# Front stage of a mixture-of-experts kernel: routing weights by row transfers instead of a matmul

## The reference, cut to what matters

```python
logits = x @ gate_weight.T                      # 16 experts
scores = sigmoid(logits)
topk_w, topk_idx = top_k(scores, 2)
topk_w = topk_w / (topk_w.sum(-1) + 1e-20)
comb = zeros((T, 16)).at[arange(T), topk_idx].set(topk_w)
g = silu(einsum('th,ehi->eti', x, We_gate))
u = einsum('th,ehi->eti', x, We_up)
ye = einsum('eti,eih->eth', g * u, We_down)
y = einsum('te,eth->th', comb, ye)              # + the shared expert
x = x + 0.5 * (y + shared)
```

## Time and profile before

| | us |
|---|---|
| median of 3 runs | 2211.61 (2210.7 to 2214.48) |
| time of the profiled execution | 2212.05 |
| span of its trace | 2210.3 |
| PE busy | 1984.1 (90%) |
| DVE busy | 1650.0 (75%) |
| ACT busy | 1083.3 (49%) |
| POOL busy | 585.6 (26%) |

### The profile page before, as it was taken

One profiled execution on the slowest core, in us unless ns is written; L12 is line 12 of the kernel. 1 busy time (PEld: TensorE's weight loads), 2 busy tenths in 40 slices (PEclk: granted clock), 3 DMA queues, 4 the chain that ended last, 5 costly groups with the idle time before them and its releaser, 6 DMA issues. The chain is left out here.

```text
span 2210.3 us, 34280 instructions
## 1 busy us (share of the span) xinstructions
PE 1984.1 (90%) x12468; PEld 1352.9 (61%) x12468; DVE 1650.0 (75%) x4096; ACT 1083.3 (49%) x1971; POOL 585.6 (26%) x621
## 2 busy tenths in 40 slices
PE   3998999899989998989899838999999999999997
PEld 3787778777877787778777723344444444444444
DVE  5766776767676767776767518988988888889982
ACT  3333323332333233323332214777777777777775
POOL 3332333233223331333133021222222222222211
PEclk9999999999999999999999956999999999999999
DMA  3000000000000000000000022222222222222220
GB/s 119 6 11 10 1 11 10 11 1 10 11 10 1 10 11 10 1 11 11 10 1 6 5 72 81 73 81 84 78 78 78 78 87 88 78 78 78 73 73 10
DMA packets 49991, 85.81 MB, mean 39 GB/s; under 512 B 6752, under 2 KB 11104, under 8 KB 49760
## 3 DMA queue, kind: packets, MB, share of 16 engines
q1 hardware_dynamic: 47920, 81.85, 11.6%
q10 hardware_dynamic: 1904, 1.78, 0.2%
HBM read 49.26 MB, written 34.87 MB: 38 GB/s over the span
## 5 line engine op out<-in xcount | busy, mean ns | idle before, releaser
L1302 DVE TENSOR_REDUCE b_nm<-b_MX 128x1 f32<-128x512 f32 x1024 | 651.8, 683 | 80.1 <-PE b_MX L1417 71.4
L1184 ACT ACTIVATE b_pr<-b_ST 128x512 f32<-128x512 f32 x1024 | 551.7, 601 | 175.8 <-PE b_ST L1404 173.9
L383 ACT ACTIVATE s<-G 128x512 f32<-128x512 f32 x306 | 182.9, 598 | 432.3 <-PE G L685 423.2
L1417 PE MATMUL b_MX<-b_kt,b_qt 32*128 32x512 f32 x1024 | 357.7, 505 | 20.8 <-DMA b_qt<-staging 8.3
L690 PE MATMUL Y<-w_wd,h 128*128 128x128 f32 x2448 | 335.0, 281 | 8.6 <-DVE h L544 8.0
L690 PEld LDWEIGHTS Y<-w_wd,h 128*128 128x128 f32 x2448 | 315.0, 195 | 23.9 <-DVE h L544 13.4
L1404 PE MATMUL b_ST<-b_qt,b_kt 32*128 32x512 f32 x1024 | 305.8, 497 | 19.5 <-ACT b_pr L1184 18.7
L1404 PEld LDWEIGHTS b_ST<-b_qt,b_kt 32*128 32x128 f32 x1024 | 123.3, 183 | 317.0 <-ACT b_pr L1184 214.4
L535 DVE TENSOR_TENSOR su<-U,s 128x512 f32<-128x512 f32 x272 | 186.3, 685 | 160.8 <-ACT s L383 83.1
L1432 PE MATMUL b_PV<-b_pr,b_va 128*32 128x512 f32 x2048 | 276.2, 612 | 0.0
L544 DVE TENSOR_TENSOR h<-C,su 128x512 f32<-128x512 f32 x272 | 188.1, 692 | 9.3
(11 more groups left out here) (237 smaller groups left out, 3431.9 us busy)
## 6 DMA issues: line engine op xcount, KB each, us to landing
b_kt<-staging SPq DMA_DIRECT2D x64, 256.0 KB, 2.8
b_qt<-staging SPq DMA_DIRECT2D x64, 256.0 KB, 3.1
staging<-b_khi SPq DMA_DIRECT2D x32, 256.0 KB, 3.0
staging<-b_qhi SPq DMA_DIRECT2D x32, 256.0 KB, 3.0
xin<-in_x SPq DMA_DIRECT2D x17, 256.0 KB, 2.6
mid<-xo SPq DMA_DIRECT2D x17, 256.0 KB, 2.0
b_x<-mid SPq DMA_DIRECT2D x16, 256.0 KB, 2.9
staging<-b_klo SPq DMA_DIRECT2D x16, 256.0 KB, 3.1
```

The source lines that it names most:

```text
L383: nc.scalar.activation(sbuf_s[n % 2][:], G[n % 2][:], ACT.Silu).then_inc(act_done.sem, 1)
L1184: nc.scalar.activation(pr[k % 2][:, j], bank[:].rearrange("p a b -> p (a b)"), ACT.Exp, scale=SM_SCALE).then_inc(used["st"].sem, 1)
L1302: nc.vector.tensor_reduce(nm[g % 2][:, c:c + 1], bank[:].rearrange("p a b -> p (a b)"), AX.X, ALU.max).then_inc(used["mx"].sem, 1)
L1417: pe.matmul(flat(MX[place % MX_BANKS]), qt[g][rows_of(j), u // HG % T], flat(kt_[g])[rows_of(j)], start=True, stop=True).then_inc(made["mx ...
```

## The change

The rows of weights no longer come from a matmul. After the top 2, DVE writes comb alone (no split); PE transposes it one step after the step "weights" of the slot before the one that uses it; ACT copies 16 partitions of it to cT; SP writes cT to a DRAM buffer, waits, and reads it back with 16 transfers, each of which repeats one row over 64 partitions, into cw (two buffers of 8 pairs). Each pair has a semaphore of its own, reached by two transfers. C, `pairs` and the split are gone. U gets two banks, s three buffers. DVE multiplies U by cw first (su, needs no ACT), then su by s to h. For ATT slots the steps of low, logits, first, second and weights are one earlier.

```diff
-    ATT: {"statistics": 1, "transpose": 3, "low": 4, "logits": 5, "first": 6, "second": 7, "weights": 8},
+    ATT: {"statistics": 1, "transpose": 3, "low": 3, "logits": 4, "first": 5, "second": 6, "weights": 7},
...
+            def spread_weights(q, i):
+                k = number(q, i)
+                p = k % 2
+                sp.wait_ge(cT_ready.sem, cT_ready.at(i, q + 1))
+                if k >= 2:
+                    for n in range(TE):
+                        sp.wait_ge(spread[n], 32 * (k - 1))
+                sp.dma_start(spread_dram[p], cT[p][:].rearrange("e t p -> e (t p)")).then_inc(rows_out, 16)
+                if k >= 2:
+                    sp.wait_ge(h_ready.sem, NT * (k - 1))
+                sp.wait_ge(rows_out, 16 * (k + 1))
+                for n in range(TE):
+                    for e in range(2):
+                        sp.dma_start(cw[p][e * I_E:(e + 1) * I_E, n].rearrange("p t q -> p (t q)"),
+                                     spread_dram[p][2 * n + e:2 * n + e + 1].broadcast_to([I_E, N])
+                                     ).then_inc(spread[n], 16)
...
+            for i in range(turns):
+                for m in range(NM):
+                    spread_weights(m + 1, i)
+                    if m % 2 == 1:
+                        store(i, m)
+                        if i < turns - 1:
+                            load(i, m, min(i * 2 + 3 + m // 2, 2 * turns - 1 - m // 2))
...
+            def weight_rows(q, i):
+                k = number(q, i)
+                act.wait_ge(combT_ready.sem, combT_ready.at(i, q + 1))
+                if k >= 2:
+                    act.wait_ge(rows_out, 16 * (k - 1))
+                nc.scalar.activation(cT[k % 2][:], Z[0:E], ACT.Copy).then_inc(cT_ready.sem, 1)
...
-                step(nc.vector.tensor_tensor(comb[:], first[:], share[:], ALU.mult))
-                own.settle()
-                step(nc.vector.tensor_copy(combh[:], comb[:]))
-                own.settle()
-                step(nc.vector.tensor_copy(comb2[:, :, 0:E], combh[:]))
-                nc.vector.tensor_tensor(comb2[:, :, E:2 * E], comb[:], combh[:],
-                                        ALU.subtract).then_inc(comb_ready.sem, 1)
+                wait_for(dve, combT_ready, i, q)
+                nc.vector.tensor_tensor(comb[:, :, 0:E], first[:], share[:], ALU.mult).then_inc(comb_ready.sem, 1)
...
+                    dve.wait_ge(spread[n - 1], 32 * (k + 1))
+                    wait_for(dve, h_ready, i, g0 + n - 1)
+                    step(nc.vector.tensor_tensor(su[n % 2][:], U[n % 2][:], cw[k % 2][:, n - 1], ALU.mult))
+                    dve.wait_ge(act_done.sem, act_done.at(i, g0 + n + 1))
+                    own.settle()
+                    ins = nc.vector.tensor_tensor(out[:], su[n % 2][:], s[:], ALU.mult)
...
-                nc.vector.tensor_tensor(h[n % 3][:], C[:], su[n % 2][:], ALU.mult).then_inc(h_ready.sem, 1)
...
-                    if n >= 1:
-                        pe.wait_ge(up_used.sem, up_used.at(i, g0 + n))
-                    product(U, w["wuh"][:, n], w["wul"][:, n], high, low).then_inc(up_ready.sem, 1)
-                    if n == 0:
-                        comb_transposes(m, i)
-                    else:
-                        routing_weights(m, n, i)
+                    if n >= 2:
+                        pe.wait_ge(h_ready.sem, h_ready.at(i, g0 + n - 1))
+                    product(U[n % 2], w["wuh"][:, n], w["wul"][:, n], high, low).then_inc(up_ready.sem, 1)
+                    if prepare and n == steps["weights"] + 1:
+                        comb_transposes(m + 1, i)
...
             main_transposes(-1, 0)
             logits(-1, 0)
+            comb_transposes(-1, 0)
```

More of the change, by code:

```diff
@@ L104, in nth, with build_front @@
     return SIDE[:m].count(SIDE[m])
[L107 removed]
+def build_front(nc, weights, x_dram, mid_dram, ident_dram, spread_dram, turns):
     w = weights
@@ L153, in build_front @@
         den = sb("den", [P, T, 1])
[L154 to L159, removed]
+        comb = sb("comb", [P, T, P])
+        cT = [sb(f"cT{p}", [E, T, P]) for p in range(2)]
+        cw = [sb(f"cw{p}", [P, TE, T, P]) for p in range(2)]
+        sbuf_s = [sb(f"s{p}", [P, T, P]) for p in range(3)]
         su = [sb(f"su{k}", [P, T, P]) for k in range(2)]
@@ L180, in build_front @@
         G = [ps(f"G{k}", [P, T, P]) for k in range(2)]
-        U = ps("U", [P, T, P])
-        C = ps("C", [P, T, P])
+        U = [ps(f"U{k}", [P, T, P]) for k in range(2)]
         Y = ps("Y", [P, T, P])
@@ L243, in build_front @@
         oT_ready = sig("oT_ready", N_ATT)
+        spread = [ctx.enter_context(nc.semaphore(f"spread{n}")) for n in range(TE)]
+        rows_out = ctx.enter_context(nc.semaphore("rows_out"))
         comb_cleared = ctx.enter_context(nc.semaphore("comb_cleared"))
@@ L250, in build_front, with number, wait_for @@
         block = ctx.enter_context(nc.Block())
+        slots = NM * turns + 2
+        def number(m, i):
+            return NM * i + m + 1
+        def wait_for(eng, signal, i, n):
+            if signal.at(i, n) > 0:
+                eng.wait_ge(signal.sem, signal.at(i, n))
         def source(q):
@@ L275, in load @@
                 sp.dma_start(xin[p][:], xd[batch]).then_inc(x_loaded[p].sem, 16)
-            load(0, -1, 2)
[L278 to L290, removed]
+            def spread_weights(q, i):
[14 more added lines that the diff above has]
+                                     ).then_inc(spread[n], 16)
+            spread_weights(-1, 0)
+            spread_weights(0, 0)
+            load(0, -1, 2)
+            for i in range(turns):
[5 more added lines that the diff above has]
+                            load(i, m, min(i * 2 + 3 + m // 2, 2 * turns - 1 - m // 2))
             sp.wait_ge(side_done.sem, side_done.at(turns, 1))
@@ L408, in slot @@
                             scores(m + 1, i)
+                        if n == steps["weights"] + 1:
+                            weight_rows(m + 1, i)
             main_high(-1, 0)
@@ L697, in moe_down, with comb_transposes @@
                     pe.wait_ge(main_done.sem, main_done.at(i, m))
[L698 to L700 removed]
+                pe.wait_ge(h_ready.sem, h_ready.at(i, NT * m + n + 1))
                 down(Y, h[n % 3], w["wd"][:, n], n == 0).then_inc(down_done.sem, 1)
[L703 to L704 removed]
+            def comb_transposes(q, i):
+                if number(q, i) == 0:
                     pe.wait_ge(comb_cleared, 1)
[L706 removed]
+                pe.wait_ge(comb_ready.sem, comb_ready.at(i, q + 1))
                 for t in range(T):
[L708 removed]
+                    mm = pe.transpose(Z[:, t], comb[:, t], w["ident"][:])
                 mm.then_inc(combT_ready.sem, 1)
[L711 to L719 removed]
             def side_transposes(i, k):
@@ L1491, in build_weights @@
     sb("router", [P, 2 * E], F32R)
-    sb("pairs", [P, TE, P], F32R)
     for name, shape in parts.items():
@@ L1510, in build_weights @@
         router = scratch("router", [P, E])
-        pairs = scratch("pairs", [P, TE, P])
         theta_t = scratch("theta_t", [P, T, P])
```

55 lines of the change are left out of this document (16 added, 39 removed).

## The result

| | before | after |
|---|---|---|
| median, us | 2212.18 (2210.7 to 2214.48) | 2242.45 (2239.37 to 2251.32) |
| time of the profiled execution | 2212.05 | 2239.37 |
| span of its trace | 2210.3 | 2237.6 |
| PE, DVE busy | 1984.1, 1650.0 | 1945.1, 1657.5 |

The ratio is 1.0139 [1.0121, 1.0157]: 1.4% slower, at +30 us in the medians and +27.3 in the profiled executions, where +11 was forecast and the range ended at 2240.

A forecast was written before the change was run, and what follows sets the result against it. It took each slot as a chain of latencies with a full PE only between them. MLP -0.85 and ATT +1.6 made +0.75 per pair, x 16 = +12, edges -1: +11 us, 2223; range 2180 to 2240.

The forecast's parts named there:

- The chain to comb in ATT slots: ATT slots, DVE work from statistics to comb: 9.4 us from 754.15, comb ready at 763.55, PE waiting for it.
- The wait for xl ahead of the logits: ATT slot, step 4: PE stops 0.75 us for xl because the logits stand one step earlier.
- The wait ahead of U: ATT slot, step 8: PE's 2.39 us wait for the U bank goes, but returns as a wait for comb.
- The shared access, og: ATT slots: routing_second's two-SBUF-operand operations wait for POOL's two og passes, +2.0 us on the chain to comb.
- z in the MLP slot: MLP slot, step 2: h lands between POOL's z passes, so z can come 0.65 us later and PE waits.
- C and the transposes in MLP slots: MLP slot: C of steps 3 to 7 saves 1.15 us; comb transposes in step 7's full stream cost 0.35.
- The residual: MLP slot: routing_weights leaves step 8, so the residual starts 0.70 us earlier and shifts zs and z.
- The transfers: Weight rows through DRAM in the turns: hidden by 1 us or more, cost 0.
- Edges: Slot -1 +1 us, last slot -2, set-up between 0 and -1; together -1.
- the walk of the ATT slot: ATT slot followed in the new order: it ends at 767.4 as before, 0 to -0.3 us without shared access.
- Rival A: Faster: shared access costs no more than before; pair -1.8 us, 2182 us in all; chance 0.25.
- B: No change: routing_second pays for one og pass (1.1 us), z 0.65 late; 2212, 2208 to 2216; chance 0.2.

The follow-up runs named there:

- e11: Changed kernel with unread filler matmuls ahead of the comb transposes (ATT), zs transposes, and the xls and z waits of MLP slots: 2212.93 us, ratio 1.0006.
- e3: Kernel before the change with 9 unread filler matmuls in the 2.39 us wait ahead of U in step 8 of ATT slots: 2199.48 us, ratio 0.9933.
- e4: Changed kernel without the weight-row transfers, cw filled once with 0.125: 2245.18 us, ratio 1.0139.
- e9: Changed kernel with comb transposes behind ATT slots moved into the next slot, old ATT steps, and xls ahead of su and h in MLP step 1: 2202.31 us.
- e8: Changed kernel with 16 unread matmuls ahead of the comb transposes of ATT slots and 7 ahead of the zs transposes of every slot: 2234.12 us, ratio 1.0097.
- e2: Changed kernel with 16 unread filler matmuls ahead of the comb transposes of ATT slots: 2215.29 us, ratio 1.001.
- r3: e8 repeated, on the same chip as r2: 2229.94 us, ratio 1.0084.
- r2: e2 repeated on a further chip: 2222.47 us, ratio 1.0043.
- e1: Changed kernel with routing_second ahead of out_normalise in ATT slots: 2232.2 us, ratio 1.0088.

## Why the prediction was wrong in size

The direction was right. The mechanism that I named is there, and at full clock the slots lose what I forecast, +12 us. But it is half of the loss: another +14 comes from the clock of PE, which the sum didn't have. In all +27.3 us between the profiled executions for +11. Point by point:

- *The chain to comb in ATT slots* (forecast: PE waits 3 to 4 us, transposes 35.1 after the residual): right. 3.99 us and 35.04; from the statistics to the end of comb 11.22 for 11.4. The wait for xl ahead of the logits is 0.61 for 0.75. The wait ahead of U is gone.
- *The shared access, og* (+1.6, bounds 0 to 2.0): right in kind, and close to its upper bound. L526 and L529 take 0.82 + 1.09 = 1.91 more. The ATT slot up to its next G is 1.8 longer at full clock (e11: transposes at 35.09, G 3.59 later, 38.68; before 767.37 - 730.50 = 36.87). The Trainium skill's "SBUF — State Buffer", "Who interferes with whom", says that a DVE instruction with two SBUF inputs and a GpSimd one that reads SBUF shut each other out for the whole instruction. The trace agrees: L529 of 64 columns ends with the pass of 512.
- *z in the MLP slot* (+0.65): wrong, it cost nothing. The z transposes stand 10.34 after the residual before and after (705.67 - 695.33; 801.72 - 791.38). POOL's second pass ran its 1.04 unhindered and DVE's h gave way, where nothing waited for it. DVE of after, then POOL:

```profile
800.73 1.49 DVE L564 TENSOR_TENSOR h<-su,s 128x512 f32<-128x512 f32 x1
```

```profile
800.62 1.04 POOL L339 TENSOR_TENSOR z<-z,rstd 128x512 f32<-128x512 f32 x1
```

- *C and the transposes in MLP slots* (-1.15 + 0.35 = -0.80): -0.71, right.
- *The residual* (-0.70): right in kind, it follows the down product in all slots, but mis-sized at full clock. I took it from the slot that ends at 695 us, which is one with the clock down, and walked the other. From G to the residual it is 0.62 before (767.99 - 767.37) and 0.28 after: -0.34.
- At full clock these make 1.8 - 0.34 - 0.71 = +0.75 per pair, which is the forecast's +0.75 and the +0.77 of e11 less e3. The equality is luck: z was too dear by 0.65, the residual too good by 0.36, og too cheap by 0.2.
- *The transfers* (0): right, by e4, with a margin of some 4 us instead of 1 (above). The two landings take 1.6 and 3.0 where I had put 3.1 for each. Edges (-1): the last slot gave -2.2 as forecast; start and back moved by +7.2 and -3.0, of which most shows without the change too.
- **What failed: the walk of the ATT slot took one slot for all and one clock for both kernels.** Nine ATT slots of before take 39.05, not 37.49, by the clock after the 2.39 us wait; that stood in the trace. I forecast that the 2.39 would be replaced by a wait of 3 to 4 us, priced it by its length only, and let the slot end "763.95 + 3.45" as before. The 3.45 from the out_transposes to the next G took 4.67 (866.02 - 861.35): behind the wait of 3.99 the clock falls in every ATT slot of after. In the mean that is 1.68 per ATT slot (40.65 - 38.97) where before paid 0.86. Difference 0.82 x 16 = +13.1. With start, last slot and back at +2.0 instead of -1 (+3.0), this is the missing 16.
- Rival A (faster) fell because the shared access did cost what its rows said; B (no change) because both og passes were paid for, not one. None of the rivals had the clock as its mechanism.

What stays open: why the clock falls behind the 2.39 of one ATT slot of before and not behind that of the next, and in some executions of e9 more often than in others. That the fall goes away when the waits are filled is shown in both orders; the rule by which the chip decides is not.

## What to carry to other kernels

Walk more than one instance of a repeating stage, and read the granted clock of each: two lengths of the same stage with the same waits are the sign that the clock is at stake. A wait of PE in a stream that is otherwise full is priced by its length and by what the clock does behind it; where it can't be removed, a few matmuls into a tile that nobody reads at that moment can be worth more than the edit that one was about to make (12.9 us in the kernel before). Fill all such waits, or look where the fall goes: in after the fall was free where PE would have waited anyway. When work is taken from PE that fills a latency, nothing is gained, and the latency is now idle.

## What the hardware showed that I had not expected

- PE is 91% busy in before from 60 to 660 us and still loses its clock. It fell behind waits of 2.39 (before), of 1.0 (e9) and of 1.05 and 0.68 us (e8), in streams that also have other waits. A single fall stays at 0.50 for between 3 and 4 us. What it costs depends on where it stands: 1.56 at the end of an ATT slot of before, 1.6 at 10.5 us into an MLP slot (e2, e8), 0.9 behind the zs wait of an ATT slot and nothing behind that of an MLP slot (both after).
- Filling one wait can move the fall to the next: e8 and r3, with more filled, are slower than e2 and r2 (1.0097 and 1.0084 against 1.001 and 1.0043). Only with all of them filled (e11) is it gone. The Trainium skill's "TensorE: Matmul & The Clock Gate", section "HAM oscillation — how this bites in real kernels", tells of a kernel that waits 3 to 5 us for each of its blocks and starts every one at the lower clock. The trace agrees in kind, with the 3.99 of after; the falls behind waits of 1 us are not in that section.
- Of two engines that want the shared access, POOL's z pass was served first when it started 0.11 ahead of h (800.62, 800.73); h lost 0.8 us. In e1 both sides lost: h 1.19 instead of 0.69, and POOL's second pass 1.59 instead of 1.26.
